# The opening of layer 0 in a two-layer post-norm transformer kernel: weights in five transfers, a new send order, twelve products of ones on TensorE

## The reference, cut to what matters

```python
qkv = x @ w_qkv                                  # (2, 1024, 256) @ (256, 768)
q, k, v = split(qkv), 16 heads of 16
dots = einsum('bhid,bhjd->bhij', q, k) * scale   # causal mask above the diagonal
attn = softmax(dots); out = attn @ v; out @ w_out + b_out
```

## Time and profile before

| what | value |
| --- | --- |
| median of 3 runs | 994.31 us (993.94 to 997.31) |
| profiled execution, its own time | 996.74 us |
| its span, first to last instruction | 995.0 us |
| PE busy | 944.1 us, 95% of the span |
| mean granted clock of TensorE | 0.984 |

### The profile page before, as it was taken

One profiled execution on the slowest core, in us unless ns is written; L12 is line 12 of the kernel. 1 busy time (PEld: TensorE's weight loads), 2 busy tenths in 40 slices (PEclk: granted clock), 3 DMA queues, 4 the chain that ended last, 5 costly groups with the idle time before them and its releaser, 6 DMA issues. The chain is left out here.

```text
span 995.0 us, 18001 instructions
## 1 busy us (share of the span) xinstructions
PE 944.1 (95%) x6514; PEld 510.5 (51%) x6514; DVE 685.0 (69%) x1525; ACT 593.2 (60%) x1212; POOL 382.1 (38%) x444
## 2 busy tenths in 40 slices
PE   6979999999998999988999999999999998999997
PEld 3533333333355887643334434343434353898896
DVE  2668888888854675678888888888888543434423
ACT  3457777777755334626677777777777767322321
POOL 2353333224423453416435445262624333333432
PEclk9989999999999999979899999999999999999999
DMA  6855222210000200342605233040401000000001
GB/s 209 286 169 150 65 66 65 65 41 26 2 1 20 77 1 9 101 130 80 192 12 169 90 90 115 23 137 1 138 2 40 2 1 1 1 1 22 22 1 43
DMA packets 34084, 66.30 MB, mean 67 GB/s; under 512 B 6159, under 2 KB 22431, under 8 KB 31620
## 3 DMA queue, kind: packets, MB, share of 16 engines
q1 hardware_dynamic: 32652, 60.56, 19.7%
q0 software_dynamic: 1072, 3.80, 1.1%
q10 hardware_dynamic: 272, 0.79, 0.2%
HBM read 52.55 MB, written 12.32 MB: 65 GB/s over the span
## 5 line engine op out<-in xcount | busy, mean ns | idle before, releaser
L1175 ACT ACTIVATE prob<-ps 128x512 f32<-128x512 f32 (+6 forms) x896 | 426.8, 541 | 160.1 <-PE ps L1220 157.0
L1220 PE MATMUL ps<-qop,kop 98*128 98x512 bf16 (+14 forms) x1376 | 271.5, 288 | 3.3 <-DMA qop<-mrow 2.0
L1206 PE MATMUL ps<-kop,qop 96*128 96x512 bf16 (+3 forms) x896 | 243.2, 358 | 12.2 <-DVE maxes L1105 10.7
L1220 PEld LDWEIGHTS ps<-qop,kop 107*128 107x128 bf16 (+1 forms) x1376 | 113.1, 97 | 214.2 <-ACT prob L1175 118.9
L1249 PE MATMUL ps<-prob,vst 128*32 128x512 f32 (+4 forms) x1792 | 211.2, 543 | 5.2 <-POOL prob L1039 2.9
L1105 DVE CUSTOM_DVE_ANT_0 sums<-ps,tri 128x128 bf16<-128x128 f32 (+7 forms) x256 | 180.5, 754 | 30.2 <-PE ps L1206 27.8
L1039 POOL TENSOR_TENSOR prob<-prob,keep 128x384 int32<-128x384 int32 (+2 forms) x144 | 121.7, 853 | 189.0 <-ACT prob L1175 188.6
L1105 DVE CUSTOM_DVE_ANT_0 sums<-ps,table 128x960 bf16<-128x960 f32 x128 | 148.0, 1157 | 47.9 <-PE ps L1206 35.5
L1655 PE MATMUL ps<-xs,wffn 128*128 128x512 f32 x640 | 156.1, 396 | 1.2 <-PEq L844 1.2
L1105 DVE CUSTOM_DVE_ANT_0 tri<-ps,table 128x960 bf16<-128x960 f32 x128 | 147.6, 1153 | 5.3 <-PE ps L1206 5.3
L1550 POOL TENSOR_TENSOR hs<-hf,hs 128x512 fp32r<-128x512 f32 x64 | 82.9, 1296 | 151.3 <-ACT hs L1573 142.7
(11 more groups left out here) (106 smaller groups left out, 701.8 us busy)
## 6 DMA issues: line engine op xcount, KB each, us to landing
table<-in_table SPq DMA_DIRECT2D x32, 464.0 KB, 4.7
qop<-q_parts SPq DMA_DIRECT2D x96, 128.0 KB, 2.6
kop<-k_parts SPq DMA_DIRECT2D x48, 128.0 KB, 2.6
kop<-k_parts SPq DMA_DIRECT2D x48, 96.0 KB
q_parts<-qop SPq DMA_DIRECT2D x8, 384.0 KB, 2.8
q_parts<-kop SPq DMA_DIRECT2D x8, 384.0 KB, 2.7
prob<-in_xt SPq DMA_DIRECT2D x4, 512.0 KB, 8.1
x<-in_x SPq DMA_DIRECT2D x4, 512.0 KB, 5.7
```

The source lines that it names most:

```text
L1175: nc.scalar.activation(prob[0:rows, q % 2, k % HG, lo % CH:lo % CH + hi - lo], ps[0:rows, home["exp", n, k], lo % CH:lo % CH + hi - lo], A ...
L1206: last = nc.tensor.matmul(ps[:, S_BANK + score_slot(L, k)[0] + a // CH, a % CH:a % CH + b - a], qop[0:RD, par, h, i0:i0 + P], kop[0:RD, pa ...
L1220: return nc.tensor.matmul(ps[:, bank, a % CH:a % CH + b - a], lhs, rhs, start=start, stop=True, skip_group_check=True)
```

## The change

The weights come in five transfers on ScalarE's queue: column blocks 0 and 2 (128 KB each, w_loaded), then 1, 3 and the 256 columns of v on a semaphore shared with the identity, for which v step 0 waits. Twelve f32 products of the 128 x 128 tile of ones run on PE ahead of unit 0, their output unused. The load of group 1 moves ahead of units 8 to 11 in SP's queue, and send_rows(0) ahead of units 14 and 15. In the last steps of the list v 7 stands before finish 15. POOL stages group 0's values after maximum 16 of the opening, not at its end.

```diff
+WARMING = 12
@@ opening_of
-    last = len(behind) - (1 - layer.index)
+    last = len(behind) - 2 * (1 - layer.index)
...
         out.append(("max", n, 1))
+        if layer.index == 0 and n == len(units) // 2:
+            out.append(("stage", 0, 1))
@@ Projection.steps(1)
-                    u[5], f[4], v[2], u[6], f[5], u[7], f[6], f[7], v[3]]
+                    u[5], f[4], v[2], u[6], f[5], u[7], f[6], v[3], f[7]]
@@ Projection.pe
+                if k == 0:
+                    pe.wait_ge(self.ident_and_w, 16 * 4)
...
-                pe.wait_ge(self.w_loaded, 16 * (1 + i))
+                pe.wait_ge(self.w_loaded, 16 * 2)
@@ sync
-            later = len(proj.units) // 2 + 4 * (1 - i)
+            later = len(proj.units) // 2
...
-            for u in range(later, len(proj.units)):
+            ahead_of_rows = len(proj.units) - 2 * (1 - i)
+            for u in range(later, ahead_of_rows):
                 proj.send(sp, u)
             send_rows(0)
+            for u in range(ahead_of_rows, len(proj.units)):
+                proj.send(sp, u)
@@ gpsimd
+                        if n == 0:
+                            pool.wait_ge(proj.v_done, TB)
...
-            pool.wait_ge(proj.v_done, (8, 1)[i])
-            stage(0, 0)
+            if i == 1:
+                pool.wait_ge(proj.v_done, 1)
+                stage(0, 0)
@@ scalar
-                act.dma_start(proj.w[:], dram.wq[0].rearrange("(k p) n -> p k n", p=P)).then_inc(proj.w_loaded, 16)
+                wv = dram.wq[0].rearrange("(k p) n -> p k n", p=P)
+                for m in (0, KD):
+                    act.dma_start(proj.w[:, :, m * P:(m + 1) * P], wv[:, :, m * P:(m + 1) * P]).then_inc(proj.w_loaded, 16)
+                for m in (1, KD + 1, 2 * KD):
+                    width = P if m < 2 * KD else D
+                    act.dma_start(proj.w[:, :, m * P:m * P + width], wv[:, :, m * P:m * P + width]
+                                  ).then_inc(proj.ident_and_w, 16)
@@ tensor
+            if i == 0:
+                pe.wait_ge(proj.ones_set, 1)
+                for _ in range(WARMING):
+                    nc.tensor.matmul(ps[:, SIDE, 0:P], K.ones[:], K.ones[:], start=True, stop=True)
```

More of the change, by code:

```diff
@@ L330, in __init__ @@
         self.x_loaded = [sem(f"x_loaded{c}") for c in range(NC)] if i == 0 else None
-        self.ident_loaded = sem("ident_loaded") if i == 0 else None
+        self.ident_and_w = sem("ident_and_w") if i == 0 else None
         self.w_loaded = sem("wqkv_loaded" + tag)
@@ L916, in _ @@
                     load_turned(c)
-                sp.dma_start(K.ident[:], dram.ident).then_inc(proj.ident_loaded, 16)
+                sp.dma_start(K.ident[:], dram.ident).then_inc(proj.ident_and_w, 16)
                 operands.constants(sp, 0)
@@ L1313, in step @@
                         if i == 0 and n == 0 and k == 0:
-                            pe.wait_ge(proj.ident_loaded, 16)
+                            pe.wait_ge(proj.ident_and_w, 16 * 4)
                         pe.wait_ge(evicted, n * 2 + (k + 1))
```

## The result

The changed kernel has a median of 998.67 us (996.22 to 1001.13, 9 runs), against 995.48 us (993.14 to 997.31, 9 runs) for the kernel before on the same chips: ratio 1.0035, 95% interval 1.0019 to 1.005. The change made the kernel some 3.2 us slower, where 7.1 us faster was forecast.

What follows compares the result with a forecast made beforehand. PE, busy 95% of the span, was taken as the bound, with group 0's start deciding. Terms -2.9 + 0 - 1.2 - 3.0 = -7.1 us gave 987.2 us on the median (989.6 against the profiled execution); range 984.0 to 992.5.

Steps and rivals of the forecast that it cites:

- step 4: Raw weights and ScalarE: raw mostly precedes group 1's early load, so ScalarE's chain comes 2.6 us earlier (-2.9 + 0.3).
- My rival: Queues share, group 1's load delays raw to 49.3 us: gain only 4.3 us, 990.0 us; chance 0.20 with the clock up.
- The slower rival: Group 1's load and sends behind it hold raw until all gains are outweighed: 0.8 us slower, 995.1 us; chance 0.03.
- Step 1: Warm-up and units 0 to 3: products of ones raise the clock, 16 records take 7.04 us, not 9.93: -2.9 us.
- Step 2: The opening's term between warm-up and scores, judged by unit 0's start under the split weight transfers: 0 us.
- The early weights: Case of weights landing early, unit 0 starting at 6.5 us: 985.6 us in all; chance 0.12.
- Step 3: The scores: both chains start at unit 0 and shorten by 2.9 us, first score at 30.5 us.
- Step 5: The rows' gate: with v 7 ahead of finish 15, the transpose no longer waits for v 7's copy: -1.2 us.
- Step 6: From mrow's copy to the first exponential: SP free for the rows, 3.7 us in place of 6.7: -3.0 us.
- the half-clock stretch behind the exponential: PE's low-clock work after the first exponential: nothing counted, since the clock likely falls as today; up to 1.8 us otherwise.

Runs made afterwards that it cites:

- load1_back: The changed kernel with the load of group 1 back behind units 8 to 11's sends; 991.16 us, ratio 0.9953 to the kernel before.
- load1_behind_raw: The changed kernel with group 1's load behind units 8 and 9's sends and after the raw weights' landing; 991.62 us, ratio 0.9954 to the kernel before.
- back_one_transfer: The changed kernel with group 1's load back behind units 8 to 11 and w in one transfer; 992.11 us, ratio 0.9975 to the kernel before.
- half_early: The changed kernel with only the queries of group 1's load early, its keys behind units 8 to 11's sends; 995.03 us, ratio 0.9995 to the kernel before.
- order_alone: The kernel before with only v 7 ahead of finish 15 and the row sends ahead of units 14 and 15's sends; 992.52 us, ratio 0.9975.
- no_products: The changed kernel without the twelve products of ones; 999.75 us, ratio 1.0035 to the kernel before.
- load1_alone: The kernel before with only the load of group 1 moved ahead of units 8 to 11 in SP's queue; 1001.83 us, ratio 1.0048.

## Why the prediction was wrong

**The step that failed is 4**, "What is queued first goes first". I took two stretches in which only one queue moved for a rule, against the equal sharing of the earlier trace rows, which I had in hand. In the changed kernel load 1, most of whose issues came after raw's, moved beside raw; its DMA queues from 42 to 50 us:

```profile
DMA packets 545, 2.18 MB, mean 273 GB/s; under 512 B 151, under 2 KB 151, under 8 KB 406
...
q1 hardware_dynamic: 273, 1.13, 54.0%
q0 software_dynamic: 271, 1.04, 48.0%
```

273 packets of SP's queue against 271 of POOL's. Raw gets 1.04 MB in these 8 us. Here the bytes are nearly equal too. That it is the packets that were equal, and not the bytes, is shown from 52 to 53 us, where SP's queue holds the sends' 1 KB packets and raw's are of 4 KB:

```profile
q0 software_dynamic: 74, 0.30, 78.9%
q1 hardware_dynamic: 77, 0.08, 24.5%
```

The numbers are not equal in every stretch: from 53 to 54 us, as raw comes to its end, they are 186 of SP's against 58 of POOL's.

The wait that I had read in the earlier trace rows is real, but it is not an order of whole transfers. In load1_back unit 8's send, issued at 40.28 us, moves no packet before 43.0 us either, at least 2.7 us after its issue, where unit 0's send in the kernel before, with nothing beside it, was issued at 16.61 us and moved 159 packets between 17.5 and 18.0. Why a send begins later beside raw is not shown by any run.

Without load 1 beside it, raw has the engines to itself; load1_back from 38 to 41 us:

```profile
DMA packets 327, 1.25 MB, mean 415 GB/s; under 512 B 23, under 2 KB 23, under 8 KB 327
...
q0 software_dynamic: 327, 1.25, 102.4%
```

That is 0.42 MB per us against the 0.13 of the 8 us beside load 1 (1.04 / 8).

**The price of sharing was mis-sized too.** My rival gave load 1 its bytes at raw's speed, 3.9 us, and so 49.3 us for raw. It was 54.99. The reason is in the same two rows: the engines together moved 273 GB/s and not 415, though busy (54.0% and 48.0%). A raw packet took 0.480 x 16 x 8 us / 271 = 0.23 us there and 1.024 x 16 x 3 / 327 = 0.15 us alone. Load 1's transfers are slow by themselves: in load1_behind_raw, from 48 to 56 us (193 packets of 8 KB and 193 of under 512 B), SP's queue is practically the only busy one (load 1, and at the end a send) and still moves 1.70 MB in 70.7% of the engines' time, 1.70 / (0.707 x 8) = 0.30 MB per us of busy time, against raw's 1.25 / (1.024 x 3) = 0.41. With units 8 and 9's sends behind it (they landed after 12.4 and 11.8 us, 6.5 and 5.1 before), SP's queue beside raw was never empty: in each 2 us from 42 to 54 us it moved 67 packets or more. Which property of these transfers makes them slow was not tried.

**The slower rival was the right one**, at a chance of 0.03. Its point of decision was raw landing 5.1 us later than today: it landed 6.7 later, by its own rule 1.6 us to be lost, and the first exponential was 1.8 us later. I held it impossible together with a won clock, since I had bounded the delay by bytes.

Of step 4 the consequence was right: ScalarE's chain behind raw, not PE, sets the time of v 7's copy and with it the maxima's end.

**Step 1** (-2.9 us) is right in its size and not dependable; that load1_back's trace shows all of it is in part luck. Its 5.4 us are the stretch of the six slow records in the earlier trace rows, from 8.14 to some 13.5 us (by their 1088 ns against 611 the clock was at half there, though the windows of that trace print it as 1.00); its 7.04 us held, the 16 records of units 0 to 3 spanning 7.03 to 7.13 us where all are fast. The step took the products to run at half clock to their end. But the clock can rise inside them, and the moment differs: with the same 12 products their records turned from 421 to 275 ns at about 4 us in back_one_transfer, between 4 and 5 us in the changed kernel, and between 5 and 6 us in load1_behind_raw and half_early. In load1_back all 24 took 421 ns to the end at 6.5 us and unit 0's first records, from 8.18 us on, were fast: there the clock rose only behind the products. The earlier the rise, the earlier the 12 products end and the longer PE pauses: they end at 5.4 us in back_one_transfer (pause 2.63 us), at 5.7 in the changed kernel (2.56), at 6.1 and 6.3 in load1_behind_raw and half_early (2.05 and 2.02) and at 6.5 in load1_back (1.64). Units 0 to 3 took 7.13 us with 12 products (pause 1.64 us) and with 17 (1.48 us); 8.52 to 8.83 us in four executions with 12 products (pauses of 2.02 to 2.63 us); 8.59 to 10.07 us in five without any. That these pauses are what lost the clock fits the seven traces with products, one of each kernel, but the pause was not varied by itself. On the total no number of products made a difference that these intervals resolve: 0.9953 (12), 0.9971 (17), 0.9981 (24), 0.997 (none).

**Step 2** (0) was right within half a microsecond: unit 0 starts at 8.18 to 8.55 us in the seven traces with five transfers whose products were over by then, and at 7.97 to 8.14 us in the four with one transfer. The small pieces win nothing and may cost 0.1 us or more. The reading of near equal numbers of packets, and so of equal bytes until the first weights are there, fits this: from 3 to 6.5 us load1_back's queues moved 396 (weights) and 436 packets. The early weights that the forecast counts at 0.12, with unit 0 at 6.5 us and 985.6 us in all, from which the lower end of its range is taken, are a term that no run shows: unit 0 never started before 7.97 us.

**Step 3** was right for unit 3 (its sends moved by what step 1 gave) and in load1_back also for the first score: 31.01 us, 2.4 us early.

**Step 5** (-1.2 us) was right: the parts release the transpose, in order_alone for 1.4 us. In no_products and half_early v 7's copy comes last all the same, but only some 0.2 us behind the parts.

**Step 6** (-3.0 us, 3.7 us from mrow's copy to the exponential) came out in full only where load 1 is issued before the last sends: 3.4 us lie between the transpose and the first exponential product in the changed kernel and in load1_behind_raw, against 7.0 before. With load 1 in its old place 4.9 to 6.3 us lie between them (load1_back 5.9, order_alone 6.2). And in load1_alone, with load 1 early and the old order of the rows, it is 4.3. By this comparison 2.7 us come from SP being done with load 1, and 0.9 us from the row sends' new place.

**The sum.** Without step 4's error the opening gives 5.0 us in load1_back's trace and 4.7 us by its ratio (0.9953 of 996.41); I had forecast 7.1. In that trace the transpose is at 61.82 us, 3.9 us early (4.1 by steps 1 and 5), and the exponential follows 5.9 us later, not the 4.0 of step 6: load 1's issues and two sends hold the rows until 64.11 us and the six maxima's operands with them. These 1.9 us are the price of load 1's old place. In four of the five traces with 12 products part of step 1 is missing as well. For the half-clock stretch behind the exponential I had taken nothing: from the first exponential product to the row send of the next group 25.5 us pass in the kernel before, 25.2 in the changed kernel and 24.7 in load1_back, so up to 0.8 us was to be had there.

In the medians the changed kernel lost 3.2 us where its profiled execution shows 1.5 to 1.8 us in the opening. That execution is among the fastest of nine. The three near 996 us have a mean granted clock of 0.983 to 0.987, the six from 998.36 to 1001.13 us one of 0.979 to 0.985, so more time at the lower clock goes with the longer executions; where they spend it was not traced.

The best versions are load1_back (991.16 us, 0.47% under the kernel before) and load1_behind_raw (0.46% under it), which these runs cannot tell apart. order_alone holds 0.25% in two edits.

## What to carry to other kernels

A load that is moved earlier must be priced by what it then runs beside, not only by who waits for it: here nobody used group 1's operands for 37 us after the load's first issue (34.18 to 71.44 us), and the raw weights beside them were what ScalarE waited for. A bound in bytes was not enough for it (3.9 us by bytes; against the kernels with load 1 back or behind raw it was 8.7): take the slower transfer's own packets, and the sends queued behind it. For work that is to raise TensorE's clock, look at the pause between its end and the first real product: here the clock was up through units 0 to 3 after pauses of 1.48 and 1.64 us and was not after those of 2.02 to 2.63 us. The same 12 products ended between 5.4 and 6.5 us, the earlier the sooner the clock rose in them. And the clock is worth only what that product's chain carries to the end: no number of products made a difference in the total that these intervals resolve.

## What the runs showed of the hardware that was not expected

SP's and POOL's queues, side by side, moved nearly equal numbers of packets and not of bytes (77 of 1 KB against 74 of 4 KB from 52 to 53 us of the changed kernel), and beside load 1's transfers the two together moved 273 GB/s (42 to 50 us) where POOL's alone moved 415 (38 to 41 us of load1_back). TensorE's clock rose after 3 to more than 5 us of small products of ones, not at the same moment with the same products: records of 421 ns turned to 275 ns at about 4 us in back_one_transfer, and in load1_back, with as many products, all took 421 ns until their end at 6.5 us. It had fallen again after a pause of 2.56 us with nothing on PE (changed kernel, 0.50 from 8.3 us on), while it survived one of 1.48 us (17 products: records of 275 ns ahead of the pause, units 0 to 3 in 7.13 us behind it). After a pause of 2.05 us (load1_behind_raw) it was still up when unit 0 began and fell at about 9 us, within its records (0.97 from 8.2 to 9.0 us, 0.50 from 9.0 to 12.0). In executions without products the number of slow records differs too (units 0 to 3 took 8.59 us in order_alone and 10.07 in no_products).
